# Running the gate of each token tile right after the tile's normalization, in one loop

## The reference

```python
xn = _layernorm(x, axis=-1)
x = x + attn(xn, Wq, bq, ..., Wo, bo, scale) + ffn(xn, gate_w, gate_b, expert_w, expert_b)

def _layernorm(x, axis=-1, eps=1e-5):
    m = jnp.mean(x, axis=axis, keepdims=True)
    v = jnp.var(x, axis=axis, keepdims=True)
    return (x - m) / jnp.sqrt(v + eps)

# attn: 16 heads of 64, rotary embedding on q and k, causal softmax, output projection
# ffn, the part that matters here:
gate_logits = jax.nn.softmax(x @ gate_w + gate_b, axis=-1)      # 8 experts
selected = (gate_logits >= THRESHOLD).astype(x.dtype)           # 0.1
weights = gate_logits * selected
weights = weights / jnp.where(wsum == 0, 1, wsum)               # wsum = sum(weights)
for e in range(E):
    out = out + weights[:, e:e + 1] * (x @ expert_w[e] + expert_b[e])
```

## Time and profile before

| | us |
|---|---|
| median of 3 runs | 3396.26 (3395.76 to 3396.36) |
| profiled execution | 3396.03 |
| its span on the slowest core | 3394.5 |
| spans of the 8 cores | 3375.1 to 3394.5 |
| TensorE busy | 2543.7 (75%) |
| VectorE busy | 1088.1 (32%) |
| ScalarE busy | 1106.2 (33%) |
| GpSimd busy | 189.1 (6%) |

### The profile page before, as it was taken

How to read it: one execution, slowest core, us unless ns; L and a number is a source line. 1 busy time by engine, 2 the same in 40 slices (tenths; PEclk the granted TensorE clock), 3 DMA queues, 4 the chain that set the end, 5 groups by cost and what they waited for, 6 DMA issues and landing times.

```text
span 3394.5 us, 34611 instructions; the slowest of 8 cores (3375.1 to 3394.5 us)
## 1 busy us (share of the span) xinstructions
PE 2543.7 (75%) x11560; PEld 997.4 (29%) x11720; DVE 1088.1 (32%) x1902; ACT 1106.2 (33%) x2608; POOL 189.1 (6%) x365
## 2 busy tenths in 40 slices
PE   1169777897774499799931796779977745996999
PEld 1124222342221144244411342223422212442443
DVE  2347200372002244234343571004710032442443
ACT  3212687425874000000042127783267730000000
POOL 2000000000000100100000000000000001001000
PEclk9999887997876699899965898789977767998999
DMA  5031100110000322322230211001000003224222
GB/s 128 25 47 32 18 5 4 17 18 3 4 6 3 75 38 38 114 48 38 53 110 12 47 32 19 5 4 18 17 3 5 4 3 87 38 38 124 38 38 62
DMA packets 41820, 120.23 MB, mean 35 GB/s; under 512 B 8486, under 2 KB 8616, under 8 KB 36784
## 3 DMA queue, kind: packets, MB, share of 16 engines
q0 software_dynamic: 32432, 101.24, 14.4%
q1 hardware_dynamic: 9216, 16.78, 1.3%
HBM read 157.84 MB, written 16.78 MB: 51 GB/s over the span
## 4 chain that ended last, share of the span: by engine, by line
PE 60%; ACT 17%; DVE 10%; issue 6%; DMA 5%; POOL 2%; DVEq 1%; ACTq 0%; POOLq 0%; SPq 0%
PE P L688 30%; PE P L381 12%; ACT s_ptA L560 6%; PE P L548 5%; ACT s_ptB L563 5%; PE P L574 4%; PE P L579 3%; PE P L555 2%; DMA s_ws<-wex 2%; DMA s_UB<-x 1%; ACT s_onT L593 1%; DVE s_t1b L445 1%; DVE s_t2b L448 1%; DVE s_onT L652 1%; DVE s_t1b L450 1%
## 5 line engine op out<-in xcount | busy, mean ns | idle before, releaser
L688 PE MATMUL P<-s_ws,s_xnT 128*128 128x512 bf16 x4012 | 888.4, 382 | 111.2 <-DMA s_ws<-wex 106.8
L381 PE MATMUL P<-s_xnT,s_ws 128*128 128x512 bf16 x2496 | 578.3, 384 | 37.7 <-DMA s_ws<-wvn 29.0
L709 DVE SCALAR_TENSOR_TENSOR s_UB<-P,s_wcol,s_UB 128x512 f32<-128x512 f32 x512 | 384.3, 751 | 615.5 <-PE P L688 615.5
L688 PEld LDWEIGHTS P<-s_ws,s_xnT 128*128 128x128 bf16 x4096 | 402.5, 98 | 597.1 <-issue 121.2
L574 PE MATMUL P<-s_ptA,s_UB 128*65 128x512 bf16 (+3 forms) x640 | 270.1, 422 | 259.8 <-ACT s_ptB L563 254.7
L560 ACT ACTIVATE s_ptA<-P,s_negmh 128x512 bf16<-128x512 f32 (+3 forms) x640 | 397.3, 621 | 159.8 <-PE P L555 102.9
L563 ACT ACTIVATE s_ptB<-P,s_negmh 128x512 bf16<-128x512 f32 (+3 forms) x640 | 394.4, 616 | 0.0
L548 PE MATMUL P<-s_UB 64*128 64x512 bf16 (+3 forms) x1280 | 350.7, 423 | 1.9 <-DVE s_negmh L522 1.9
L381 PEld LDWEIGHTS P<-s_xnT,s_ws 128*128 128x128 bf16 x2560 | 242.3, 99 | 332.0 <-issue 60.8
L579 PE MATMUL P<-s_ptB,s_UB 128*65 128x512 bf16 (+3 forms) x640 | 271.9, 425 | 0.0
L414 DVE SCALAR_TENSOR_TENSOR s_t1b<-P,s_bkp,s_Ct 128x512 f32<-128x512 f32 x64 | 48.0, 751 | 587.0 <-PE P L381 582.0
(11 more groups left out here) (110 smaller groups left out, 1614.7 us busy)
## 6 DMA issues: line engine op xcount, KB each, us to landing
s_ws<-wex POOLq DMA_DIRECT2D x36, 1024.0 KB, 8.3
s_UB<-x POOLq DMA_DIRECT2D x32, 512.0 KB, 3.8
s_UB<-x POOLq DMA_DIRECT2D x64, 256.0 KB, 6.9
out<-s_UB SPq DMA_DIRECT2D x64, 256.0 KB, 2.0
s_ws<-wqp POOLq DMA_DIRECT2D x16, 256.0 KB, 4.4
s_ws<-wqs POOLq DMA_DIRECT2D x16, 256.0 KB, 5.1
s_ws<-wkp POOLq DMA_DIRECT2D x16, 256.0 KB, 6.3
s_ws<-wks POOLq DMA_DIRECT2D x16, 256.0 KB, 7.1
```

Source lines behind the costliest of these rows:

```text
L381: t.matmul(psum[:, 0:512], sl[:, woff + fc * 128: woff + (fc + 1) * 128], xnT[:, fc * L + win * 512: fc * L + (win + 1) * 512], start=(fc ...
L688: t.matmul(bank[:, 0:512], src[:, fc * L + tt * 128: fc * L + (tt + 1) * 128], wslot[slot][:, fc * 512:(fc + 1) * 512], start=(fc == 0), s ...
L709: v.scalar_tensor_tensor(asl, bank[:, 0:512], wcol[:, tt * 8 + e: tt * 8 + e + 1], asl, op0=ALU.mult, op1=ALU.add), inc="sv")
```

## The change

The gate loop is dissolved. Its body stands at the end of the body of the normalization loop, so that tile tt is normalized and gated before tile tt + 1 is begun. The barrier between the two loops is gone. In its place TensorE waits, before the gate products of a tile, for the eviction of this tile into `xnT` (the value `xnev_tt`). Banks, buffers and operations are the same.

```diff
@@ -316,12 +316,12 @@
                                     bank[:, :].bitcast(BF16)[:, fc * 128:(fc + 1) * 128], AI),
                       inc="ss" if fc == NFC - 1 else None)
             rel[("xnev", s, tt + 2)] = em.val("ss")
-
-        if phases < 2:
-            continue
-        em.barrier()
-        for tt in range(NT):
+            xnev_tt = em.val("ss")
+
+            if phases < 2:
+                continue
             bank = P[2]
+            em.wait_val("t", "ss", xnev_tt)
             em.wait_val("t", "ss", rel.get(("gate", s, tt), 0))
             for fc in range(NFC):
                 em.op("t", lambda t, fc=fc, tt=tt, bank=bank:
```

## The result

The changed kernel takes 3546.8 us (median of 10 executions) where the kernel before took 3396.8 in the same rounds. The ratio is 1.0441, with a 95% interval of 1.0430 to 1.0453: 4.4% slower. The forecast was 3546.

The account below looks back on a forecast made before the run. Normalization and gate were taken as bound by hand-offs between engines. Fifteen periods of 14.09 us plus a last tile of 14.49 make 225.8 us a sequence, +149.8 us over both: 3546 us, range 3528 to 3564.

Parts of the forecast that it names:

- The path of one tile: Fused loop: hand-offs from BN_STATS through the eviction into xnT and wbf to the next BN_STATS, 13.97 us.
- The allowance of 0.12 us for late hand-offs: Fused loop: 0.12 us added to each tile, ends 0 and 0.16, giving a period of 14.09 us.
- The loads: Fused loop: Sqrt and Exp displace each other's table in each tile; 60 more exposed loads, 1283 ns each, 77 us.
- The overlap: Fused loop: BN_STATS of the next tile waits behind wbf on VectorE; lost overlap, net of vanished x waits, 73 us.
- The cover of wT: Tile end: transposing wbf and evicting into wT stays off the path, with 1.9 us of cover left before Sqrt.
- x: Loads of x in the fused loop: 22 us available for each, so waits after the first tile vanish.
- "Hidden" loads: Rival: table loads move ahead of the waits, under BN_STATS and the gate's products; 3469 us, 5%.
- "dearer" loads: Rival: every switch costs more than its load row, by a drain or doubled load; 3634 or 3628 us, 4%.
- The faster side: Rival: the gate of tile tt fills holes in normalizing tile tt+1, 6.0 us a tile; 3286 us, 2%.
- both terms: Loss in the fused stages: 77 us of table loads and 73 us of lost overlap between neighbouring tiles.
- a sign against its size: Stages behind the fused ones: the size is wrong if they change by more than a few us.

Follow-up runs that it names:

- both edits: Changed kernel with statistics of tile tt+1 written ahead of the gate of tile tt, and Sqrt replaced by Identity: 3407.9 us, ratio 1.0024 to the kernel before.

## Why the prediction was right

- **The path of one tile.** Forecast 13.97 us, measured 13.96 at the first boundary; mean of 15 periods (31.19 to 242.12) 14.06, forecast 14.09. The allowance of 0.12 us for late hand-offs was 0.10. The stages came out at 225.4 and 225.1 us, forecast 225.8.
- **The loads.** 64 at 1283 ns, all behind their waits. Taking them out gives 77 us (80.7 in the two stages, where 63 rows make 80.8), hiding them gives 77, adding 60 to another program costs 61 in its stages, since 0.75 us of idle time there take part of each pair. The drain that the Trainium skill adds ("ScalarE: Activation LUTs", "What ACT_TABLE_LOAD costs") doesn't show behind busy work either: 0.01 us. In this kernel a switch costs 1.28 us behind an idle ScalarE, as all 64 stand here, 1.41 behind a busy one, and in neither case 2.66.
- **The overlap.** The prediction put 73 us on it. Writing the statistics ahead gives 54 us back (56 in the stages), and with both edits the kernel is 0.24% above before. In the stages, 148.7 us of loss are 80.7 of loads (63, of which three stand in the kernel before too), 56.4 of statistics, 4.3 by which both edits give more than the two alone, and 7.3 that stay.
- **The cover of wT.** 1.87 us of idle ScalarE stand in the changed kernel, 1.9 forecast. When the statistics no longer hid it, its end became the start of the next switch, at the price worked out beforehand.
- **x.** VectorE waited for x only twice, 38.0 us in all, at the first tile of each sequence, as forecast.
- **The rivals.** "Hidden" loads fell with the idle ScalarE ahead of each load and with the gain that hiding them gave; "dearer" loads fell with the runs that took loads out and added them. The faster side would have needed stages under 151.2 us; even with both terms taken away the first took 155.4.
- **Luck.** A miss of 0.8 us is closer than the working deserves. The stages came out 1.1 us under the forecast, the runs of before moved from 3396.3 to 3396.8, and the second remainder differs between cores by up to 11 us within the profiled execution.
- **What stays open.** The 6.4 us behind the second stage on the profiled core. The prediction named a change of more than a few us there as a sign against its size. The other cores scatter around no change (-2.9 to +6.3 us), and the medians don't ask for it: 3546.8 - 3396.8 = 150.0, and the stages give 148.7. One thing did change behind both stages: on this core the granted clock in the second 100 us from the first projection on is 0.82 and 0.83, where before has 0.88 twice. The first remainder is no longer than before in spite of it, so it isn't shown to cost anything. No run tells why it fell.

## What to carry to other kernels

Joining two loops on in-order queues is not overlap: each engine gets the second loop's work in front of the next tile of the first, and what one stage used to start early is lost. Write down what stands behind what on each queue, add the hand-offs once around, and compare with the sum of the two periods. On ScalarE also count the changes between functions that displace each other's table; if the order can't be changed, an activation of a constant that waits for nothing pulls the load into idle time, and small operations on 8 columns for each tile can be done once for all tiles, which took this kernel from 3547 to 3267 us.

## What was not expected of the hardware

Between back-to-back instructions a table load has 0.01 us of gap in front of it and 0.01 behind it, and no drain; what it adds beyond its own 1283 ns is only the 0.10 us by which the two activations around it would have overlapped. And a transfer issued early isn't free: 1.25 MB of weights behind each of x tiles 3 and 8 made the next x tiles take 11.7 and 11.2 us to land, where 4 is usual, and took back all the gain that can be seen.
